# A decoder layer on one core: the maxima of the self attention from 64 rows, two heads in the row halves of TensorE

## The reference

```python
q, k, v = proj(WQ), proj(WK), proj(WV)          # 16 heads of 16
q, k = rope(q), rope(k)
scores = einsum('bhqd,bhkd->bhqk', q, k) / sqrt(16)
scores = where(causal, scores, -inf)
attn = softmax(scores)
out = einsum('bhqk,bhkd->bhqd', attn, v)
return out @ Wo.T + Wo_b
```

## Time and profile before

| | |
|---|---|
| runs | 1228.73, 1233.89, 1232.59 us, median 1232.59 |
| profiled execution | 1232.33 us, span 1230.4 us |
| first stage | 0 to 83 us of the span |
| self attention | 83 to 547.5 us |
| TensorE, VectorE, ScalarE busy over the span | 84%, 72%, 48% |

### The profile page before, as it was taken

One profiled execution on the slowest core, in us unless ns is written; L12 is line 12 of the kernel. 1 busy time (PEld: TensorE's weight loads), 2 busy tenths in 40 slices (PEclk: granted clock), 3 DMA queues, 4 the chain that ended last, 5 costly groups with the idle time before them and its releaser, 6 DMA issues. The chain is left out here.

```text
span 1230.4 us, 17963 instructions
## 1 busy us (share of the span) xinstructions
PE 1030.9 (84%) x6184; PEld 510.9 (42%) x6184; DVE 884.8 (72%) x1794; ACT 585.0 (48%) x805; POOL 286.3 (23%) x268
## 2 busy tenths in 40 slices
PE   8528999999999999976399967989989877889970
PEld 4312333333333333234278841332323216778860
DVE  5727998888899888307369989988878833755545
ACT  1311456666666666762244312755556552323322
POOL 6630101121021100116300016522010012332225
PEclk9855999999999999997799966999989987999995
DMA  5450189900000000013111003411111001242225
GB/s 191 142 145 1 22 83 105 103 2 1 1 2 1 2 1 1 2 32 114 39 52 52 1 23 130 128 41 55 33 34 42 19 33 45 66 146 66 75 73 175
DMA packets 60265, 70.04 MB, mean 57 GB/s; under 512 B 10316, under 2 KB 53708, under 8 KB 60172
## 3 DMA queue, kind: packets, MB, share of 16 engines
q1 hardware_dynamic: 54652, 57.40, 19.8%
q0 software_dynamic: 3408, 9.34, 2.1%
q10 hardware_dynamic: 2112, 2.10, 0.5%
HBM read 45.37 MB, written 22.85 MB: 55 GB/s over the span
## 5 line engine op out<-in xcount | busy, mean ns | idle before, releaser
L601 DVE TENSOR_REDUCE self_piece_max<-self_max 128x1 f32<-128x512 f32 (+3 forms) x640 | 349.5, 604 | 46.2 <-PE self_max L503 25.4
L568 ACT ACTIVATE self_probs<-self_scores 128x1024 f32<-128x1024 f32 (+3 forms) x320 | 274.1, 896 | 193.7 <-PE self_scores L522 192.8
L503 PE MATMUL self_max<-stack_k,stack_q 96*128 96x512 bf16 (+3 forms) x640 | 209.4, 365 | 6.2 <-DVE self_piece_max L601 3.4
L1733 DVE TENSOR_REDUCE cross_piece_max<-banks 128x1 f32<-128x512 f32 x256 | 164.0, 683 | 27.9 <-PE banks L1624 25.9
L1701 ACT ACTIVATE cross_probs<-banks 128x1024 f32<-128x1024 f32 x128 | 126.4, 1022 | 108.6 <-PE banks L1647 106.7
L522 PE MATMUL self_scores<-stack_q,stack_k 98*128 98x512 bf16 (+3 forms) x640 | 170.6, 350 | 4.4 <-DMA stack_q<-self_shift 3.1
L533 PE MATMUL self_out<-self_probs,V 128*17 128x512 f32 (+3 forms) x1280 | 148.8, 537 | 2.6 <-ACT self_probs L568 2.0
L503 PEld LDWEIGHTS self_max<-stack_k,stack_q 96*128 96x128 bf16 x640 | 62.2, 98 | 173.6 <-DVE self_piece_max L601 131.1
L469 POOL TENSOR_SCALAR_AFFINE_SELECT self_probs<-self_probs 128x512 f32<-128x512 f32 x64 | 40.6, 634 | 399.1 <-ACT self_probs L568 398.8
L1624 PE MATMUL banks<-kx_few,stackx 97*128 97x512 bf16 x256 | 97.4, 420 | 22.9 <-DVE cross_piece_max L1733 14.0
L1647 PE MATMUL banks<-stackx,kx_few 99*128 99x512 bf16 x256 | 80.1, 398 | 1.2 <-ACT cross_probs L1701 0.6
(11 more groups left out here) (317 smaller groups left out, 1575.7 us busy)
## 6 DMA issues: line engine op xcount, KB each, us to landing
stack_q<-qparts SPq DMA_DIRECT2D x96, 64.0 KB, 9.1
stackx<-xparts SPq DMA_DIRECT2D x96, 64.0 KB, 2.3
xin<-sent SPq DMA_DIRECT2D x39, 129.0 KB, 2.1
stack_k<-kparts SPq DMA_DIRECT2D x18, 256.0 KB, 14.9
qparts<-parts SPq DMA_DIRECT2D x8, 384.0 KB, 2.6
kparts<-parts SPq DMA_DIRECT2D x8, 384.0 KB, 3.0
xparts<-xparts_sb SPq DMA_DIRECT2D x8, 384.0 KB, 2.8
o_tok<-in_w SPq DMA_DIRECT2D x4, 768.0 KB, 5.1
```

The source lines that it names most:

```text
L503: mm = nc.tensor.matmul(slot[:, 0:pc["w"]], pc["lhsT"], pc["rhs"], start=True, stop=not pc["diag"])
L568: nc.scalar.activation(probs[:, i % 3, 2 * pair:2 * pair + 2, st["off"]:C], ps[:, 2 * pair:2 * pair + 2, st["off"]:C], ACT.Exp, scale=SCAL ...
L601: nc.vector.tensor_reduce(piece_max[:, u % 2, pc["row"], pc["at"]:pc["at"] + 1], slot[:, 0:pc["w"]], AX.X, ALU.max).then_inc(side_read, 1)
L1733: nc.vector.tensor_reduce(piece_max[:, u % 2, pc["row"], pc["at"]:pc["at"] + 1], slot[:, 0:pc["w"]], AX.X, ALU.max).then_inc(side_read, 1)
```

## The change

Five edits, all in the first stage and the self attention:

1. The pairs of parts are put in the order (0,0), (0,1), (1,0), (1,1), (0,2), (2,0). The maxima use the first four alone: 64 rows instead of 96.
2. Heads 0 and 1 of a group have these in partitions 0 to 63, heads 2 and 3 in 64 to 127 (`stack_row`); their last two pairs lie in 0 to 31, their shift in rows 32 and 33, and the rest of 32 to 63 holds ones against zeros, so their scores go over 128 rows. Every load is split in two: 24 transfers for a chunk instead of 12, 36 for a later group instead of 30, and four for a shift instead of two; GpSimd sets three areas for each chunk instead of one.
3. Pieces come in pairs, one of a lower and one of an upper head. Both buffers are waited for first, then both matmuls are issued, then the masks.
4. `schedule` moves pairs: EVEN = 2 pairs a step, the first after the first scores, the second after the second scores, none after the values (three pairs: one in each).
5. `parts` has eight buffers and two semaphores. The load of the last chunk is issued behind the first shift.

```diff
-PAIRS = [(0, 0), (0, 1), (1, 0), (0, 2), (2, 0), (1, 1)]
+PAIRS = [(0, 0), (0, 1), (1, 0), (1, 1), (0, 2), (2, 0)]
+SLOTS = 8
-EVEN = 4
+EVEN = 2
...
+            def stack_row(n, half):
+
+                return (n * DK + HALF * half) % P
...
-                                    if n >= 4:
-                                        act.wait_ge(s_parts_out[n % 4], 16 * (n // 4))
-                                    nc.scalar.copy(parts[:, n % 4, 0], whole[:, n % 4]).then_inc(p1_ready, 1)
+                                    if n >= SLOTS:
+                                        act.wait_ge(s_parts_out[n // 4 % 2], 16 * TC * (n // SLOTS))
+                                    nc.scalar.copy(parts[:, n % SLOTS, 0], whole[:, n % 4]).then_inc(p1_ready, 1)
...
-                                for to, there in stack_pairs(0, c - 1, c)[(n % 4 - 1) * 4:n % 4 * 4]:
+                                for to, there in stack_loads(0, c - 1)[(n % 4 - 1) * 8:n % 4 * 8]:
...
+                thirds = []
+                for groups in side:
+                    thirds.append([[], [], []])
+                    for n, group in enumerate(groups):
+                        thirds[-1][n if len(groups) == 2 else 3 * n // len(groups)] += group
...
+                            def free_slot():
                                 n = len(freed)
                                 if n >= SB:
                                     pe.wait_ge(*freed[n - SB])
-                                slot = pm[:, n % SB]
+                                return pm[:, n % SB]
+
+                            def maxima(u, k):
+                                made = []
+                                for pc in works[u]["pieces"][k:k + 2]:
...
+                                    slot = free_slot()
+                                    reads[0] += 1
+                                    freed.append((side_read, reads[0]))
+                                    made.append((pc, slot))
+                                done = [nc.tensor.matmul(slot[:, 0:pc["w"]], pc["lhsT"], pc["rhs"], start=True, stop=not pc["diag"])
+                                        for pc, slot in made]
+                                for n, (pc, slot) in enumerate(made):
+                                    if pc["diag"]:
+                                        done[n] = nc.tensor.matmul(slot[:, pc["w"] - P:pc["w"]], ident_b[:], tri_b[:], start=False, stop=True)
+                                    done[n].then_inc(side_ready, 1)
...
-                                pieces.append(dict(w=b - a, lhsT=stack_q[g][0:KS, c, j, q * P:(q + 1) * P],
-                                                   rhs=stack_k[g][0:KS, j, a:b], row=j * GH + q, at=n,
+                                pieces.append(dict(w=b - a, lhsT=stack_q[g][halves[half], c, j, q * P:(q + 1) * P],
+                                                   rhs=stack_k[g][halves[half], j, a:b], row=j * GH + q, at=a // C,
...
-                            keys=lambda j, g=g, kt=kt: stack_k[g][0:KS + 2, j, kt * P:(kt + 1) * P],
+                            keys=lambda j, g=g, kt=kt: stack_k[g][0:(KS + 2, P)[j // HH], j, kt * P:(kt + 1) * P],
```

More of the change, by code:

```diff
@@ L191, in decoder_layer @@
                 s_ones = sem("ones_set")
[L192 removed]
+                s_parts_out = [sem(f"parts_out{i}") for i in range(2)]
                 qk_ready, qk_read = sem("qk_ready"), sem("qk_read")
@@ L345, in schedule @@
                 for u, work in enumerate(works):
-                    stream += [("piece", u, k) for k in range(len(work["pieces"]))]
-                    stream.append(("turn", u))
+                    stream += [[("piece", u, k), ("piece", u, k + 1)] for k in range(0, len(work["pieces"]), 2)]
+                    stream.append([("turn", u)])
                 order, late = [], []
-                for item in stream:
-                    if item[0] == "turn" and item[1]:
-                        late.append([3, item])
+                for group in stream:
+                    if group[0][0] == "turn" and group[0][1]:
+                        late.append([2, group])
                         continue
-                    order.append(item)
+                    order.append(group)
                     for w in late:
@@ L362, in schedule @@
                     first_of.setdefault(st["unit"], i)
-                where = {item: n for n, item in enumerate(order)}
-                before = order[:where[("turn", 0)] + 1]
-                due, at = [], len(before)
+                where = {group[0]: n for n, group in enumerate(order)}
+                at = where[("turn", 0)] + 1
+                before = [item for group in order[:at] for item in group]
                 side = []
@@ L636, in decoder_layer @@
                 stack_k += [sb(stage, f"stack_k{g}", [P, GH, T], BF16) for g in range(1, NG)]
-                loads = [stack_pairs(0, c, c + 1) for c in range(NC)] + [stack_pairs(g, 0, NC) for g in range(1, NG)]
+                loads = [stack_loads(0, c) for c in range(NC)] + [stack_loads(g) for g in range(1, NG)]
+                halves = [slice(HALF * half, HALF * (half + 1)) for half in range(2)]
                 steps, works = [], []
@@ L657, in decoder_layer @@
                             unit=u, off=off, diag=int(kt * P >= c * C), first=kt == 0, last=kt == (c + 1) * C // P - 1,
-                            keys=lambda j, g=g, kt=kt: stack_k[g][0:KS + 2, j, kt * P:(kt + 1) * P],
-                            queries=lambda j, g=g, c=c, off=off: stack_q[g][0:KS + 2, c, j, off:C],
+                            keys=lambda j, g=g, kt=kt: stack_k[g][0:(KS + 2, P)[j // HH], j, kt * P:(kt + 1) * P],
+                            queries=lambda j, g=g, c=c, off=off: stack_q[g][0:(KS + 2, P)[j // HH], c, j, off:C],
                             values=lambda j, g=g, kt=kt: V[:, kt, g * GH + j, :]))
-                attention("self", stage, [(steps, works)], None, [stack_k[g][KS:KS + 2, :, c * C:(c + 1) * C] for g in range(NG) for c in range(NC)], loads, [],
+                attention("self", stage, [(steps, works)], None, [stack_sets(g, c) for g in range(NG) for c in range(NC)], loads, [],
                           lambda u: o_unit(*chunks[u]), True)
```

120 lines of the change are left out of this document (68 added, 52 removed).

## The result

| | before | after |
|---|---|---|
| runs, median | 1232.35 us (4 runs, 1228.73 to 1233.89) | 1304.75 us (4 runs, 1303.54 to 1305.74) |
| ratio, 95% interval | | 1.0591 [1.057, 1.0613] |
| span of the profiled execution | 1230.4 us | 1303.7 us |
| self attention in it | 83.0 to 547.3: 464.3 us | 86.7 to 618.3: 531.7 us |

The forecast was 1264 us, range 1236 to 1290: the direction is right, the loss more than twice as large (72 us for 32) and outside the range. Of it 3.7 us are the first stage and 67.4 the self attention; the last 2 lie behind them.

What follows compares the result with a forecast made beforehand. TensorE was taken as the bound from 150 to 503 us, VectorE's reads from 97 to 122. Terms -6 + 35 + 1.2 + 2.5 = +32.7 on 1232.33 us gave 1265, stated as 1264, range 1236 to 1290.

Steps and rivals of the forecast that it cites:

- TensorE's own work: -6: Self attention: pairs side by side save 57 us, 520 more changes of manner at 0.098 us add 51.
- Rival A: Self attention: changes of manner are free for row halves, but waits for the buffer grow; 1240 us, chance 0.14.
- B: Self attention: changes free and a 64-row piece appears 0.1 us sooner, shortening 186 waits; 1222 us, chance 0.12.
- C: Self attention: the halves don't run side by side, a pair takes 0.44 us; 1287 us, chance 0.14.
- Rival C's second half: Self attention: both halves run as full-array matmuls without any change of manner; 1263 us, within the forecast; no separate chance.
- The steady wait: Self attention: a step's second pair waits until VectorE has read the first pair's first piece, 0.30 us each.
- 149 places have one block of scores between two pairs: Self attention: 100 with a plain first pair wait 35.9 us in all, 49 with a mask 10.6 us.
- Sum 70, which takes the place of the 35 above.: Self attention: new buffer waits total 70 us and replace 35 us already lying with the pieces; plus 35.
- The 37 places with nothing between: Step 0 and work 0's pieces: TensorE's own work is 0.225 us against VectorE's 1.16; 21 us of waits.
- Rival D: Self attention: the granted clock may stay at 0.50 beyond 122 us; 1295 us and up, chance 0.07.
- First stage: +2.5: First stage: SyncE issues 72 loads for 36, its queue ending at 82.5 us; plus 2.5, bounds minus 6 and plus 5.
- Shift +1.2: Shift at work 0: four transfers for two, where TensorE already waits 3.1 us for the landing; plus 1.2 us.

Runs made afterwards that it cites:

- full array and early works alone: Changed kernel with pairs over the full array, second pair behind the values, one wait per pair, works 0 to 3 piece by piece: 1257.43 us, ratio 1.0193.

## Why the forecast was right and where it failed

**TensorE's own work: -6.** Right, as far as the runs can tell. The mechanism and both prices hold: halves side by side (starts 3 to 6 ns apart), 0.1 us a change. The trace has 839 changes for 318, 521 more where the forecast had 520. The sum itself can't be read from one row, since the waits cover it. The 10.3 us above belong to another order of the pairs, with 537 changes for 240 from step 20 to 140; by the forecast's prices that would be 42 us less streaming and 29 more for changes, so 13. The Trainium skill, page "TensorEngine Tiling (Array Packing)", section "Tiling Modes", says that a switch of mode drains the array; the 0.32 for 0.22 of the timeline agrees. Rival A (1240), B (1222) and C fell: the distances are 0.32, not 0.22 or 0.44. Rival C's second half, that full-array pairs without changes are as good, came true in its reasoning (ratio 1.0607 for 1.0591) and was wrong in its time like the forecast itself.

**The steady wait.** Right in kind and place, on the read of the first pair: 163 waits in all, 103 of them, 40.9 us, between step 20 and 140. They are fewer than the 149 forecast and longer, 0.40 us for 0.30. "149 places have one block of scores between two pairs": 46.5 us, minus 6 of own work, is 40.5; measured from step 20 to 140 are 40.1. That they agree is partly luck: the 46.5 are for all steps, and the waiting instruction, 11.6 us of it (17.1 less the 5.5 before step 20), was not in the 1.16 us of VectorE's way. The distance from pair to pair is 1.26.

**"Sum 70, which takes the place of the 35 above."** This is the step that failed. I took the 35 us as a stock of waits of TensorE from which the new ones are paid. But they were never read as waits: they are what was left of 464.3 us after 414 of work and 15 of other things. In the trace of before the maxima wait for VectorE only 3.4 us, in after 71.6: 68.2 more, so that the 70 held (with the waiting instruction in it) and the minus 35 did not. Part of the 35 is no idle time at all. From 97.1 to 121.8 us TensorE has by the forecast's prices 11.0 us of work at the full clock, so some 22 of the 24.7 at 0.50 (an estimate), while VectorE is busy as well. Nor could TensorE's idle time there pay for anything. Up to step 20 VectorE is busy 82.3 of 87.3 us, and each pair adds up to 0.57 us in which it stands idle. TensorE's waits had to be priced where TensorE is the bound, and VectorE's idle time where VectorE is. The 37 places with nothing between cost up to 0.57 each, at most 21 us, with nothing to subtract (over the full array the pairing of works 0 to 3 costs 15.3). Without the subtraction the sum would be -6 + 70 + 1.2 + 2.5 = 67.7, on 1232.33 us: 1300, against 1304.75.

The early 30.7 us, taken apart by the runs: first stage 3.7; pairing in works 0 to 3 15.3 (25.0 less 9.7, of which 4.6 fall before step 0); the second wait 5.5; the remaining 6 are the landing of the shift (1.6) and, argued but not tried, the plan, which has 7 reads more behind it by step 20 (167 for 160 VectorE instructions in the stretches above; 3 us by their lengths). The parts come from different kernels, so they add up only roughly. The 15.3 above all is a price over the full array: in row halves single pieces won only 3.3 us, or nothing, because they pay for more changes instead.

**The clock.** Rival D had 0.07 and did happen in part: 0.50 up to 137 us and again from 140.5 to 161. It has a share in the early loss, argued from the rows of step 0 and not shown by a run: at 0.50 a pair outlasts the read that covers it, where single pieces in three buffers did not. With full array and early works alone the clock was full from 127.1 us on. The forecast's 8 us for it were a bound on the waits. What the half clock costs by itself wasn't settled, since the fillers take time of their own.

**First stage: +2.5.** Right: +3.7; SyncE's queue all but without a gap, and its last issue at 84.3, 82.5 in the forecast. **Shift +1.2**: measured 1.6. **The chances**: slower 0.75 was well placed; the range ended at 1290 since the worst case of the waits was half clock alone. The ends of that term should have held the case that nothing is subtracted, +70.

## What to carry to other kernels

Count the buffers before the matmuls: a pair that takes two of three leaves the reader with nothing while it is filled, and a pair's second wait on the same semaphore costs an instruction of its own (0.1 us) unless the higher count is waited for alone. Waits that exist already are no credit against new ones: ask in each stretch which engine is full, and price the change by the idle time it gives to that one. Row halves cost a change of manner each way (0.1 us); here, with mostly one pair at a time, 10 us came back in the 120 steps in which the streaming alone would have given 42. Several pairs behind one change would need more buffers and were not tried. Nor was a fourth buffer: scores, output and the three buffers already take 8 x 512 values of a partition in PSUM, as much as any stage of this kernel. Of all versions only before with the eight part buffers was faster than before (0.9955).

## What the runs showed of the hardware

- Two waits on one semaphore ahead of one pair gave a separate waiting instruction (51 ns) in TensorE's queue: from the end of the read to the weights' load 0.12 us instead of 0.05 or 0.06, and 17.1 us over the kernel.
- Two matmuls in the row halves start 3 to 6 ns apart. The Trainium skill, page "TensorE: Matmul & The Clock Gate", Part 3, gives about 4 ns; the trace agrees.
- Going from the full array to 64 rows and back costs 0.10 us each way, as at the column strips.
- The granted clock came back in full at 161.0 us instead of 121.8 (from 126 to 161 us TensorE was busy 26.5 of 35), and earlier in parts when filler matmuls kept it busy. It fell once more from 236.1 to 239.5 us, in a stretch with TensorE busy 10.5 of 14 us, and from 239.5 us on, with TensorE busy 89%, it held to the end of the self attention.
